# Attention: maxima and scores issued to TensorE in pairs instead of one by one

## The chip, the cores and the metric

One core of a Trainium2 chip. The metric is the device time of one execution of the whole kernel in microseconds; three executions of the kernel before gave 4830.11 to 4836.53 us.

## What is computed

Two layers on a batch of 2 x 2048 tokens of width 512. Only the attention of the first layer is changed; the mixture of experts before and after it and the second layer are not.

```
q = (x @ q_w.T).reshape(b, s, HEADS, HEAD_DIM).transpose(0, 2, 1, 3)
k = x @ k_w.T
v = x @ v_w.T
scores = jnp.einsum('bhqd,bkd->bhqk', q, k) * SCALE
attn = jax.nn.softmax(scores.astype(jnp.float32), axis=-1).astype(q.dtype)
out = jnp.einsum('bhqk,bkd->bhqd', attn, v)
```

There are 16 heads of 32, and all heads share one set of keys and values. b is 2, s is 2048.

## The kernel before

The program is a sequence of stages written out per engine, with semaphores set by hand: experts, projection, `attention_stage` (L1125), output, experts, feed-forward, key-value mixing, feed-forward. `attention_stage` works on 128 queries and 8 heads at a time, which the code calls a half; there are 2 x 16 x 2 = 64 halves. Softmax needs the largest score of each query and head before the exponential, so each half's scores are computed twice, in two layouts:

- A **maximum** (`maxi`, L1237) is a matmul with the queries of one head as weights and 512 keys moving. It fills one of four PSUM banks `am` (`MBANKS`). DVE reduces the bank to one column (L1386). `am_bank` (L1216) makes a matmul wait for the use of its bank four uses before: a maximum's reduction, or, where that use was a transpose, the copies out of it.
- A **turn** (L1249): once per half, the negated maxima are transposed by a small matmul into an `am` bank of their own turn in the ring; DVE copies them out (L1400, L1402, `mT_kept`), and SP puts them as two more rows beside the queries (L1197), so that the score matmul subtracts them.
- A **score** (`score`, L1224) is a matmul with 128 keys as weights and four heads of 128 queries moving. It fills one of three banks `sc` (`SBANKS`), and waits in `p_rdy` for the exponential of the score three before it. ACT computes the exponential (L1338) into a ring of eight units `pt`.
- The **values** (L1255): 16 matmuls a batch multiply the exponentials with v. **Sums** (L1264): POOL adds the units in pairs (L1373), DMAs fold them, and once per half 8 matmuls sum them over the keys (L1267). DVE takes reciprocals (L1411) and scales the output (L1418).

TensorE's order is written out by hand in a loop over batches `c` of four units (L1278). A batch consists of 8 maxima, for scores that come 28 units later (`LEAD`), and 8 scores, one by one in turn, called m0, s0, m1, s1, ... m7, s7 below, then the values of four units. 56 maxima run ahead of the first score. Four batches make a half. In one of the four, called the turned batch here, the turn stands behind m3; the other three are called plain, and one of these has the sums ahead of its values. A pair m, s or a single one of them is called a piece, and the sixteen places of the pieces in a batch are slots 0 to 15.

Of the kernel before, what the change touches and what calls it, by code (L numbers as in the profile page):

```python
# [1110 lines left out]
BATCH = 4  # L1111
SBANKS, MBANKS = 3, 4
LEAD = 28
# [11 lines left out]
def attention_stage(nc, stage, const, q_parts, kst, v, attn, o_w, w_hi, w_lo):  # L1125
# [6 lines left out]
    with ExitStack() as ctx:  # L1132
# [26 lines left out]
        PIECES_ALL = 2 * N * UNITS  # L1159
# [4 lines left out]
        def turn_due(c, i):  # L1164

            half, at = divmod(c + 3, PER_HALF)
            return half if at == 0 and i == 3 and 0 <= half < HALVES else None
# [10 lines left out]
        def slot(half, j):  # L1178

            return 2 * (half % SETS) + j if j < 2 else 2 * SETS + j - 2  # L1180

        @block.sync
        def _(sp):
            def load(x):
                n, h = divmod(x, 2)
                k = n % 2
                for r, part in enumerate((0, 0, 1)):
                    src = q_parts[part, h * HALF * HD:(h + 1) * HALF * HD, n * P:(n + 1) * P].rearrange("(h d) q -> d h q", d=HD)
                    sp.dma_start(qst[r * HD:(r + 1) * HD, k, h * HALF:(h + 1) * HALF, :].bitcast(F32), src).then_inc(q_in[k][h], 16)

            def maxima(x):

                n, h = divmod(x, 2)
                sp.wait_ge(mT_kept, x + 1)
                for part in range(2):
                    row = KROWS + part
                    sp.dma_start(qst[row:row + 1, n % 2, h * HALF:(h + 1) * HALF, :].bitcast(F32),  # L1197
                                 mT[:, part, :].bitcast(F32)).then_inc(m_in[h], 16)

            for x in range(4):  # L1200
                load(x)
            for c in range(DC):
                sp.dma_start(raw[:, c, :], o_w[:, c, :]).then_inc(w_in, 16)
            maxima(0)
            for x in range(HALVES):
                if x + 1 < HALVES:
                    maxima(x + 1)
                if x + 4 < HALVES:
                    sp.wait_ge(s_rdy, HPIECES * (x + 1))
                    load(x + 4)  # L1210

        @block.tensor
        def _(pe):
            pe.sem_inc(p_rdy, SBANKS)

            def am_bank(use):  # L1216

                k = am_slot[use]
                if k >= MBANKS:
                    kind, which = am_use[k - MBANKS]  # L1220
                    pe.wait_ge(mx_rdy if kind == "max" else mT_kept, which + 1)
                return k % MBANKS

            def score(s):  # L1224

                half, r = divmod(s, HPIECES)
                n, h = divmod(half, 2)
                kt, g = divmod(r, 2)
                if r == 0:
                    pe.wait_ge(m_in[h], n * 32 + 32)  # L1230
                pe.wait_ge(p_rdy, s + 1)
                hh = h * HALF + g * 4
                o = (n // QT) * S + kt * P
                pe.matmul(sc[:, s % SBANKS, :], kst[0:KROWS + 2, o:o + P], qst[0:KROWS + 2, n % 2, hh:hh + 4, :],  # L1234
                          start=True, stop=True).then_inc(s_rdy, 1)

            def maxi(a):  # L1237

                half, r = divmod(a, HPIECES)
                n, h = divmod(half, 2)  # L1240
                hd, block = divmod(r, KBLOCKS)
                if r == 0:
                    pe.wait_ge(q_in[n % 2][h], (n // 2) * 48 + 48)
                bank = am_bank(("max", a))
                o = (n // QT) * S + block * 4 * P
                pe.matmul(am[:, bank, :], qst[0:KROWS, n % 2, h * HALF + hd, :], kst[0:KROWS, o:o + 4 * P],  # L1246
                          start=True, stop=True).then_inc(am_rdy, 1)

            def turn(half):  # L1249

                pe.wait_ge(neg_rdy, half + 1)
                bank = am_bank(("turn", half))
                pe.transpose(am[0:HALF, bank, 0:P], neg[:], const["ident"][:]).then_inc(mT_rdy, 1)

            def values(u):  # L1255
                half, kt = divmod(u, QT)
                n = half // 2
                pe.wait_ge(p_rdy, SBANKS + 2 * u + 2)
                for j in range(4):
                    ins = pe.matmul(pv[HD * j:HD * (j + 1), 0, :], v[:, (n // QT) * QT + kt, :], pt[:, u % RING, 2 * P * j:2 * P * (j + 1)],  # L1260
                                    start=(kt == 0), stop=(kt == QT - 1), skip_group_check=True)
                ins.then_inc(pv_rdy, 1)

            def add_up(half, j, first, last):  # L1264

                for i in range(4):
                    ins = pe.matmul(pv[HD * i:HD * (i + 1), 1, :], const["ones"][:, 0:HD], pairs[:, slot(half, j), 2 * P * i:2 * P * (i + 1)],  # L1267
                                    start=first, stop=last, skip_group_check=True)
                if last:
                    ins.then_inc(sum_rdy, 1)  # L1270

            def sums(half):

                pe.wait_ge(fold_in[-1], 16 * (half + 1))
                for j in range(2):
                    add_up(half, j, False, j == 1)

            for c in range(-LEAD // BATCH, BATCHES):  # L1278
                if c == 0:
                    for s in range(SBANKS):  # L1280
                        score(s)
                for i in range(2 * BATCH):
                    a, s = 2 * (c * BATCH + LEAD) + i, 2 * c * BATCH + SBANKS + i
                    if a < PIECES_ALL:
                        maxi(a)
                    if turn_due(c, i) is not None:
                        turn(turn_due(c, i))
                    if c >= 0 and s < PIECES_ALL:
                        score(s)
                if c < 0:  # L1290
                    continue
                half, at = divmod(c, PER_HALF)
                if at == 0 and half >= 1:
                    pe.wait_ge(vals_kept, half)
                if at == 1 and half >= 2:
                    pe.wait_ge(sums_kept, half - 1)
                if at == 0 and half >= 2:
                    sums(half - 2)
                for u in range(c * BATCH, (c + 1) * BATCH):
                    values(u)  # L1300
            pe.wait_ge(vals_kept, HALVES)
            sums(HALVES - 2)
            pe.wait_ge(sums_kept, HALVES - 1)
            for j in range(HPAIRS):
                pe.wait_ge(pair_rdy, RING // 2 + (HALVES - 1) * HPAIRS + j + 1)
                add_up(HALVES - 1, j, j == 0, j == HPAIRS - 1)
# [1133 lines left out]
```

## Time and profile before

| | us |
|---|---|
| median of 3 executions | 4834.5 |
| lowest, highest | 4830.11, 4836.53 |
| profiled execution, its own time | 4831.27 |
| its span | 4829.6 |
| attention, first to last score | 985.7 to 2544.0 |
| one half (four batches) in the middle of it | 24.36 |

The span is the time from the first to the last instruction that the profiler saw. Busy time is counted per engine: PE is TensorE's matmuls, PEld its weight loads, which run beside matmuls. Matmuls overlap each other too, so what tells their pace is the distance of their starts, and not their length.

### The profile page before, as it was taken

The page shows a single profiled execution, that of the slowest core. Times are in us where ns is not written, and L with a number is a line of the kernel's source. Part 1 is how long each engine was busy: PE and PEld are TensorE (multiplying, and loading weights), DVE is VectorE, ACT ScalarE, POOL GpSimd, SP SyncE. Part 2 cuts the span into 40 slices and gives each one's busy share as a digit, 9 for nine tenths or more (in the row PEclk, how much of TensorE's full clock was granted, in tenths as well). Part 3 has the DMA queues.
Part 4 walks back from the last instruction along what each step waited for, and adds up shares of the span by engine and source line. Part 5 has one row for each costly group of instructions (what it writes and reads, how often), then busy time and mean ns, then how long its engine had stood idle before and what let it go on. Part 6 is the DMA issues. An engine that isn't in the chain of part 4 may idle for free. (4 is left out here: it accounts for less than half of the span.)

```text
span 4829.6 us, 82831 instructions
## 1 busy us (share of the span) xinstructions
PE 4626.9 (96%) x27966; PEld 3477.5 (72%) x27967; DVE 2897.6 (60%) x5285; ACT 2107.7 (44%) x4111; POOL 2258.1 (47%) x1724
## 2 busy tenths in 40 slices
PE   6999996999999999999998799999899999999999
PEld 4788885666666666666656578888788877778888
DVE  6222225799999999999974722333455548754444
ACT  4222223456676666776662422222322235533222
POOL 1545433278888888888881154543111007500000
PEclk8999998999999999999999799999999999999999
DMA  7233326757777777777764733433522112250110
GB/s 220 83 93 98 93 83 213 260 104 146 148 146 147 146 146 147 147 147 147 146 135 155 231 94 122 131 119 110 179 66 70 55 51 82 70 196 27 35 35 27
DMA packets 245975, 585.69 MB, mean 121 GB/s; under 512 B 30816, under 2 KB 85088, under 8 KB 221152
## 3 DMA queue, kind: packets, MB, share of 16 engines
q0 software_dynamic: 62064, 317.23, 29.2%
q1 hardware_dynamic: 183536, 263.86, 16.7%
q8 instruction: 186, 3.05, 0.3%
q14 instruction: 189, 1.55, 0.1%
HBM read 263.27 MB, written 121.63 MB: 80 GB/s over the span
## 5 line engine op out<-in xcount | busy, mean ns | idle before, releaser
L1373 POOL TENSOR_TENSOR attend_pairs<-attend_pt 128x1024 f32<-128x1024 f32 x512 | 1259.0, 2478 | 197.4 <-ACT attend_pt L1338 197.2
L1386 DVE TENSOR_REDUCE attend_mx<-attend_am_ps 128x1 f32<-128x512 f32 x2048 | 1251.0, 678 | 124.7 <-PE attend_am_ps L1246 121.4
L1338 ACT ACTIVATE attend_pt<-attend_sc_ps 128x512 f32<-128x512 f32 x2048 | 1039.9, 618 | 285.3 <-PE attend_sc_ps L1234 285.1
L1246 PE MATMUL attend_am_ps<-attention_kst,attend_qst 96*128 96x512 f32 x2048 | 859.1, 425 | 10.2 <-DMA attend_qst<-q_parts 10.1
L1234 PE MATMUL attend_sc_ps<-attend_qst,attention_kst 98*128 98x512 f32 x2048 | 816.7, 400 | 1.5 <-ACT attend_pt L1338 1.3
L1637 PE MATMUL ffn_gu_ps<-ffn_y_hi,ffn_w 128*128 128x512 f32 (+1 forms) x1584 | 568.8, 369 | 3.5 <-DVE ffn_y_lo L1767 3.0
L1637 PE MATMUL ffn_gu_ps<-ffn_y_lo,ffn_w 128*128 128x512 f32 (+1 forms) x1584 | 569.0, 369 | 0.0
L1246 PEld LDWEIGHTS attend_am_ps<-attention_kst,attend_qst 96*128 96x128 f32 x2048 | 392.8, 192 | 239.8 <-DVE attend_mx L1386 122.8
L1260 PE MATMUL attend_pv_ps<-attend_pt,attention_v 128*32 128x256 f32 x8192 | 497.6, 384 | 0.0
L741 DVE TENSOR_TENSOR expert_ac<-expert_gu_ps,expert_gl 128x512 f32<-128x512 f32 x142 | 98.1, 691 | 640.5 <-ACT expert_gl L698 640.5
L1234 PEld LDWEIGHTS attend_sc_ps<-attend_qst,attention_kst 98*128 98x128 f32 x2048 | 389.4, 190 | 88.7 <-ACT attend_pt L1338 11.7
L1260 PEld LDWEIGHTS attend_pv_ps<-attend_pt,attention_v 128*32 128x32 f32 x8192 | 247.6, 110 | 214.1 <-ACT attend_pt L1338 46.8
L1709 ACT ACTIVATE ffn_sg<-ffn_gu_ps,ffn_gs 128x512 f32<-128x512 f32 (+1 forms) x198 | 127.2, 642 | 581.7 <-PE ffn_gu_ps L1637 581.7
L698 ACT ACTIVATE expert_gl<-expert_gu_ps 128x512 f32<-128x512 f32 x142 | 85.1, 599 | 661.3 <-PE expert_gu_ps L635 659.9
L635 PE MATMUL expert_gu_ps<-weights_hi,expert_x_hi 128*128 x1088 | 355.1, 408 | 5.8 <-DVE expert_x_lo L737 3.2
L635 PE MATMUL expert_gu_ps<-weights_lo,expert_x_hi 128*128 x1088 | 343.7, 397 | 0.0
L635 PE MATMUL expert_gu_ps<-weights_hi,expert_x_lo 128*128 x1088 | 343.4, 397 | 0.0
L1637 PEld LDWEIGHTS ffn_gu_ps<-ffn_y_hi,ffn_w 128*128 128x128 f32 x1584 | 298.4, 188 | 61.2 <-DVE ffn_y_lo L1767 3.6
L1637 PEld LDWEIGHTS ffn_gu_ps<-ffn_y_lo,ffn_w 128*128 128x128 f32 x1584 | 298.4, 188 | 57.4
L1777 DVE SCALAR_TENSOR_TENSOR ffn_hf<-ffn_gu_ps,ffn_us,ffn_sg 128x512 f32<-128x512 f32 (+1 forms) x198 | 137.0, 692 | 330.9 <-PE ffn_gu_ps L1637 323.1
L745 DVE TENSOR_TENSOR expert_a_lo<-expert_at_ps,expert_a_hi 128x512 fp32r<-128x512 f32 x142 | 98.1, 691 | 307.3 <-ACT expert_a_hi L702 307.3
L1653 PE MATMUL ffn_dn_ps<-ffn_w,ffn_h_hi 128*128 128x512 f32 x704 | 279.0, 396 | 0.0
(329 smaller groups left out, 7725.6 us busy)
## 6 DMA issues: line engine op xcount, KB each, us to landing
attend_pairs<-attend_pairs POOLq DMA_DIRECT2D x189, 1024.0 KB, 7.4
weights_raw<-experts_dram POOLq DMA_DIRECT2D x76, 512.0 KB, 4.1
ys<-expert_ob SPq DMA_DIRECT2D x142, 256.0 KB, 2.2
attend_qst<-q_parts SPq DMA_DIRECT2D x192, 128.0 KB, 3.9
yn<-route_yb SPq DMA_DIRECT2D x64, 256.0 KB, 4.1
ffn_xb<-x SPq DMA_DIRECT2D x64, 256.0 KB, 2.9
keyvalue_xb<-x SPq DMA_DIRECT2D x64, 256.0 KB, 2.8
weights_lo<-experts_dram SPq DMA_DIRECT2D x24, 512.0 KB, 9.5
```

Source lines behind the costliest of these rows:

```text
L635: ins = pe.matmul(gu[:, q, :], a, w[:, bass.ds(off + (c * WPIECE + q * H), H)], start=(c == 0 and n == 0), stop=(c == DC - 1 and n == 2))
L741: dve.tensor_tensor(ac[:, k, :], gu[:, 1, :], gl[:, k, :], ALU.mult).then_inc(ac_rdy, 1)
L1234: pe.matmul(sc[:, s % SBANKS, :], kst[0:KROWS + 2, o:o + P], qst[0:KROWS + 2, n % 2, hh:hh + 4, :], start=True, stop=True).then_inc(s_rdy, 1)
L1246: pe.matmul(am[:, bank, :], qst[0:KROWS, n % 2, h * HALF + hd, :], kst[0:KROWS, o:o + 4 * P], start=True, stop=True).then_inc(am_rdy, 1)
L1260: ins = pe.matmul(pv[HD * j:HD * (j + 1), 0, :], v[:, (n // QT) * QT + kt, :], pt[:, u % RING, 2 * P * j:2 * P * (j + 1)], start=(kt == 0) ...
L1338: act.activation(pt[:, u % RING, g * 4 * P:(g + 1) * 4 * P], sc[:, s % SBANKS, :], ACT.Exp, scale=HD ** -0.5).then_inc(p_rdy, 1)
L1373: pool.tensor_tensor(pairs[:, slot(half, j), :], pt[:, 2 * p % RING, :], pt[:, (2 * p + 1) % RING, :], ALU.add).then_inc(pair_rdy, 1)
L1386: dve.tensor_reduce(mx[:, hh, block:block + 1], am[:, am_slot["max", a] % MBANKS, :], AX.X, ALU.max).then_inc(mx_rdy, 1)
L1637: ins = pe.matmul(gu[:, k, q, 0:width], a, b, start=(c == 0 and n == 0), stop=(c == DC - 1 and n == 1))
L1653: ins = pe.matmul(dn[:, j % 2, :], a, b, start=(m == 0 and n == 0), stop=(m == IC - 1 and n == 1))
L1709: act.activation(sg[:, k, 0:n], gu[:, k, 0, 0:n], ACT.Silu, scale=gs[:, m:m + 1]).then_inc(sg_rdy, 1)
L1777: dve.scalar_tensor_tensor(hf[:, k, 0:n], gu[:, k, 1, 0:n], us[:, m:m + 1], sg[:, k, 0:n], ALU.mult, ALU.mult).then_inc(h_rdy, 1)
```

## The change

In a batch two maxima are issued and then two scores. The turn stays directly behind m3. No other engine's code is touched.

```diff
-                for i in range(2 * BATCH):
-                    a, s = 2 * (c * BATCH + LEAD) + i, 2 * c * BATCH + SBANKS + i
-                    if a < PIECES_ALL:
-                        maxi(a)
-                    if turn_due(c, i) is not None:
-                        turn(turn_due(c, i))
-                    if c >= 0 and s < PIECES_ALL:
-                        score(s)
+                for first in range(0, 2 * BATCH, 2):
+                    for i in (first, first + 1):
+                        a = 2 * (c * BATCH + LEAD) + i
+                        if a < PIECES_ALL:
+                            maxi(a)
+                        if turn_due(c, i) is not None:
+                            turn(turn_due(c, i))
+                    for i in (first, first + 1):
+                        s = 2 * c * BATCH + SBANKS + i
+                        if c >= 0 and s < PIECES_ALL:
+                            score(s)
```

On PE, in a turned batch from m2 on, before (`attend_am_ps<-attention_kst` is a maximum, `attend_sc_ps` a score, L1253 the turn):

```order
L1246 MATMUL attend_am_ps<-attention_kst,attend_qst 128x512
L1234 MATMUL attend_sc_ps<-attend_qst,attention_kst 128x512
L1246 MATMUL attend_am_ps<-attention_kst,attend_qst 128x512
L1253 MATMUL attend_am_ps<-all_ident,attend_neg 8x128
L1234 MATMUL attend_sc_ps<-attend_qst,attention_kst 128x512
L1246 MATMUL attend_am_ps<-attention_kst,attend_qst 128x512
L1234 MATMUL attend_sc_ps<-attend_qst,attention_kst 128x512
```

The same place now, from m2 to s7 and the values:

```order
L1246 MATMUL attend_am_ps<-attention_kst,attend_qst 128x512 x2
L1253 MATMUL attend_am_ps<-all_ident,attend_neg 8x128
L1234 MATMUL attend_sc_ps<-attend_qst,attention_kst 128x512 x2
L1246 MATMUL attend_am_ps<-attention_kst,attend_qst 128x512 x2
L1234 MATMUL attend_sc_ps<-attend_qst,attention_kst 128x512 x2
L1246 MATMUL attend_am_ps<-attention_kst,attend_qst 128x512 x2
L1234 MATMUL attend_sc_ps<-attend_qst,attention_kst 128x512 x2
L1260 MATMUL attend_pv_ps<-attend_pt,attention_v 32x256 x16
```

s2 has moved behind m3 and the turn; the turn is followed by two scores instead of one.

On PE, the end of a plain batch before (m6, s6, m7, s7 and the values):

```order
L1246 MATMUL attend_am_ps<-attention_kst,attend_qst 128x512
L1234 MATMUL attend_sc_ps<-attend_qst,attention_kst 128x512
L1246 MATMUL attend_am_ps<-attention_kst,attend_qst 128x512
L1234 MATMUL attend_sc_ps<-attend_qst,attention_kst 128x512
L1260 MATMUL attend_pv_ps<-attend_pt,attention_v 32x256 x16
```

And now, from m4 on:

```order
L1246 MATMUL attend_am_ps<-attention_kst,attend_qst 128x512 x2
L1234 MATMUL attend_sc_ps<-attend_qst,attention_kst 128x512 x2
L1246 MATMUL attend_am_ps<-attention_kst,attend_qst 128x512 x2
L1234 MATMUL attend_sc_ps<-attend_qst,attention_kst 128x512 x2
L1260 MATMUL attend_pv_ps<-attend_pt,attention_v 32x256 x16
```

Between the last maximum and the values stand two scores where there was one. The order on DVE, ACT, POOL and SP is the same before and after.

## Rows read from the trace of the kernel before

**Rows 1.** The page's engine shares: busy us (share of the span) x instructions.

```profile
PE 4626.9 (96%) x27966; PEld 3477.5 (72%) x27967; DVE 2897.6 (60%) x5285; ACT 2107.7 (44%) x4111; POOL 2258.1 (47%) x1724
```

**Rows 2.** Windows: length, busy of PE, PEld, DVE, ACT, POOL, clock, DMA, GB/s.

```profile
1400.00:1800.00 400.00, 400.00 (x3436) 260.85 (x3429) 368.17 (x656) 279.05 (x558) 352.73 (x181) 1.00 0.72 147
...
1504.87:1529.23 24.36, 24.36 (x213) 15.88 (x209) 22.48 (x40) 17.01 (x34) 21.53 (x11) 1.00 0.73 146
```

**Rows 3.** Groups by line, 1000 to 2400 us: busy us, mean ns | idle before, releaser.

```profile
L1386 DVE TENSOR_REDUCE attend_mx<-attend_am_ps 128x1 f32<-128x512 f32 x1840 | 1124.2, 678 | 106.3 <-PE attend_am_ps L1246 103.2
L1338 ACT ACTIVATE attend_pt<-attend_sc_ps 128x512 f32<-128x512 f32 x1840 | 934.3, 617 | 237.1 <-PE attend_sc_ps L1234 237.1
```

**Rows 4.** Timeline of a plain batch: start us, length, engine, instruction, [idle before <-releaser].

```profile
1535.35 0.50 PE L1246 MATMUL attend_am_ps<-attention_kst,attend_qst 96*128 96x512 f32 x1
1535.68 0.40 PE L1234 MATMUL attend_sc_ps<-attend_qst,attention_kst 98*128 98x512 f32 x1
1535.88 4.87 DVE L1386 TENSOR_REDUCE attend_mx<-attend_am_ps 128x1 f32<-128x512 f32 x8 [0.28 <-PE attend_am_ps L1246]
...
1536.12 4.03 ACT L1338 ACTIVATE attend_pt<-attend_sc_ps 128x512 f32<-128x512 f32 x8 [1.93 <-PE attend_sc_ps L1234]
...
1538.95 0.39 PE L1234 MATMUL attend_sc_ps<-attend_qst,attention_kst 98*128 98x512 f32 x1
...
1539.27 1.93 PE L1260 MATMUL attend_pv_ps<-attend_pt,attention_v 128*32 128x256 f32 x32
...
1541.13 0.50 PE L1246 MATMUL attend_am_ps<-attention_kst,attend_qst 96*128 96x512 f32 x1
```

**Rows 5.** Timeline of the turned batch before it.

```profile
1529.23 0.50 PE L1246 MATMUL attend_am_ps<-attention_kst,attend_qst 96*128 96x512 f32 x1
...
1529.77 2.48 DVE L1386 TENSOR_REDUCE attend_mx<-attend_am_ps 128x1 f32<-128x512 f32 x4 [1.47 <-PE attend_am_ps L1246]
...
1531.71 0.19 PEld L1246 LDWEIGHTS attend_am_ps<-attention_kst,attend_qst 96*128 96x128 f32 x1 [0.19 <-DVE attend_mx L1386]
...
1531.79 0.43 PE L1246 MATMUL attend_am_ps<-attention_kst,attend_qst 96*128 96x512 f32 x1
...
1532.48 0.28 DVE L1402 TENSOR_TENSOR attend_mT<-attend_am_ps,attend_mT 8x128 fp32r<-8x128 f32 x1
...
1532.81 0.19 PEld L1246 LDWEIGHTS attend_am_ps<-attention_kst,attend_qst 96*128 96x128 f32 x1 [0.20 <-DVE attend_mT L1402]
...
1532.89 0.42 PE L1246 MATMUL attend_am_ps<-attention_kst,attend_qst 96*128 96x512 f32 x1
...
1533.15 0.40 PE L1234 MATMUL attend_sc_ps<-attend_qst,attention_kst 98*128 98x512 f32 x1
```

**Rows 6.** Timeline of a batch of scores alone, near the end of attention.

```profile
2503.93 0.96 PE L1234 MATMUL attend_sc_ps<-attend_qst,attention_kst 98*128 98x512 f32 x3
2504.47 4.03 ACT L1338 ACTIVATE attend_pt<-attend_sc_ps 128x512 f32<-128x512 f32 x8
...
2505.12 0.19 PEld L1234 LDWEIGHTS attend_sc_ps<-attend_qst,attention_kst 98*128 98x128 f32 x1 [0.53 <-ACT attend_pt L1338]
2505.12 2.46 PE L1234 MATMUL attend_sc_ps<-attend_qst,attention_kst 98*128 98x512 f32 x5
```

**Rows 7.** Timeline of the batch with the sums: first maximum, first reductions.

```profile
1546.95 0.50 PE L1246 MATMUL attend_am_ps<-attention_kst,attend_qst 96*128 96x512 f32 x1
...
1547.59 3.07 DVE L1386 TENSOR_REDUCE attend_mx<-attend_am_ps 128x1 f32<-128x512 f32 x5
```

**Rows 8.** Windows: maxima alone ahead of the first score, and scores alone in the tail.

```profile
952.00:985.00 33.00, 32.03 (x56) 15.71 (x56) 31.38 (x55) 3.47 (x5) 4.96 (x4) 0.50 0.26 64
...
2530.37:2534.50 4.13, 3.91 (x27) 1.61 (x29) 3.25 (x5) 4.03 (x9) 3.39 (x3) 1.00 0.00 0
```

**Rows 9.** Timeline at the start of the first batch, at the lower clock.

```profile
987.81 0.63 PE L1234 MATMUL attend_sc_ps<-attend_qst,attention_kst 98*128 98x512 f32 x1
...
988.23 0.63 PE L1246 MATMUL attend_am_ps<-attention_kst,attend_qst 96*128 96x512 f32 x1
```

## Prediction

> **What bounds the kernel now.** Start with the engine shares [rows 1]: PE is busy 96% of the span, but that is an average over eight stages and says nothing about attention, the only stage that changes. Then the windows [rows 2]: between 1400 and 1800 us PE is busy for all 400 us at a granted clock of 1.00, its upper level (2.4 GHz), while DVE, the next busiest, has 368. The third view groups the attention instructions by line [rows 3]: one maximum occupies DVE for 678 ns, one exponential ACT for 617 ns. Eight of each belong to a batch. The last view, instructions in order of time, gives the answer. Four batches (one half) take 24.36 us [rows 2]: one carries the transpose (turned), three don't (plain). In a plain batch [rows 4] the first maximum starts at 1535.35, the second piece 0.33 later, and the sixteenth at 1538.95; so the slots behind the first are (1538.95 - 1535.68) / 14 = 0.2336 us apart without one hole. The values follow 0.32 behind the last piece, and the next batch 1.86 behind them. **TensorE sets the pace there, and whatever delays the last piece delays the whole kernel.** DVE and ACT only matter by the banks that they free, so the question is how close those releases come to the slots that need them.
>
> **The change part by part.** No instruction is added or removed. On DVE, ACT, POOL and SP the order is the same, and the sixteen slots of a batch hold the same work. What moves, counting slots from 0: m1, m3, m5, m7 go one slot forward (2 to 1, 6 to 5, 10 to 9, 14 to 13), s0, s2, s4, s6 one slot back (1 to 2, 5 to 6, 9 to 10, 13 to 14). If nothing waits, the cost is nothing. DMAs: the transposed maxima leave SP after the same DVE copies, and they are needed almost three batches later; the query loads wait for the last score of a half, which is far ahead of use. Both stay free; if a load lost that cover it would show as a wait of the first maximum of a half.
>
> *Prices of a wait.* A maximum waits for the reduction four bank uses before it. In the turned batch [rows 5] the first four reductions take 2.48 us from 1529.77, 0.60 apart, so the third ends at 1531.65; the weight load that needs its bank starts at 1531.71, and its matmul ends at 1531.79 + 0.43 = 1532.22. So a maximum ends no sooner than 0.57 behind its release. For scores I found no such wait between 1000 and 2400 us, so I take it from the tail, where batches hold scores only [rows 6]: the exponential of the first score starts at 2504.47, and the weight load of the score three later, which reuses the bank, starts at 2505.12, which is 0.65 later. The five scores then last 2.46 us at 0.49 each, so one ends 2.46 - 4 x 0.49 = 0.50 behind its load. A score ends no sooner than 1.15 behind the start of the exponential three before it.
>
> *Plain batch*, in us from the start of m0. A piece in slot k ends at 0.33 + 0.2336 (k - 1) + 0.40 [rows 4], slot 15 at 4.00. Now s0 is in slot 1, ends at 0.73, and its exponential starts at 1536.12 - 1535.35 = 0.77; the eight then run in one piece, 0.49 apart. s7 needs the exponential of s4, which starts at 0.77 + 1.96 = 2.73: it could end at 3.88 and ends at 4.00, 0.12 to spare. After the change s0 ends at 0.96, and the chain of exponentials starts at 1.00, one slot later. s3, in slot 7 (end 2.13), could end at 2.15; s5, in slot 11 (end 3.07), is held to 1.00 + 0.98 + 1.15 = 3.13; s7, still in slot 15, is held to 1.00 + 1.96 + 1.15 = 4.11 against 4.00. These delays are of one chain, so the largest counts and not their sum: **0.115 us**. The maxima press less: the reductions start at 0.53, the fourth ends at 0.53 + 1.80 + 0.68 = 3.01, so m7 could end at 3.58, where slot 13 ends at 3.53; the hold of s5 has moved it further already. The batch with the sums is alike: its reductions start 0.64 behind its first maximum now [rows 7], since DVE comes late from the output, but a longer batch gives DVE that time back. There are 249 batches that hold both kinds ((2048 - 56) / 8; 56 maxima run ahead), 62 of them turned. 187 x 0.115 = 21.5 us.
>
> *Turned batch* [rows 5]. The transpose takes a bank too, so m5 is bound by the third reduction and m7 by the copy that ends at 1532.48 + 0.28 = 1532.76; m7's load starts at 1532.81 and m7 at 1532.89. DVE is a running chain from the first reduction, and m0 keeps its slot, so neither release moves. m7 stays at 1532.89. Behind it stands one score now (1533.15); after the change two. **One slot, 0.23 us**, times 62 = 14.3 us. The exponentials don't bind here, since the same waits have delayed the scores.
>
> Two neighbours of one kind could run closer: three scores in a row take 0.96 us [rows 6], hence (0.96 - 0.50) / 2 = 0.23 apart against 0.2336. In the chain that binds, only the step from m0 to m1 and one of the two last would profit: about 1 us in all, left out. The sum is 21.5 + 14.3 = 35.8 us on the profiled execution's 4831.27 us, so 4867.1; that execution is 3.2 below the median of the runs, 4834.5, which becomes **4870**.
>
> **Bounds.** From below: if ACT's releases come just early enough, 0.12 of slack in a chain that I read to 0.01 at best, the plain batches cost nothing and the turned ones remain: +14.3, 4849. From above: every moved slot is exposed in every batch, 249 x 0.2336 = 58.2, 4893. I take the value in the middle because rows 6 measure the same wait in the same code.
>
> **Rivals.**
> 1. *Only the turned batches pay* (4849). For it: the plain batch misses by half a slot. Against: the tail shows the release with no slack. 10%.
> 2. *A whole slot in every batch* (4893), if the first score's late start also holds POOL or the values. Against: the values need the exponential of s4 only for their last unit, and POOL waits for ACT, not ACT for it. 10%.
> 3. *No change*: both releases are hidden by something the timeline doesn't show, so less than 9.7 us. 8%.
> 4. *Faster.* The mechanism: eight of fifteen steps in a batch now join matmuls of one kind, and each could be 0.2336 - 0.23 = 0.004 shorter or better. The waits would have to vanish as well: it decides from the point where exponential and reduction release their banks 0.12 us sooner than rows 5 and 6 say. Then 249 x 8 x 0.004 = 8 us, and with 0.008 per step 16 us: 4819. For it: a score behind a score has the shorter step in rows 6. Against: the chain of exponentials runs from s0 whatever PE does, so PE would only arrive sooner and wait. 4%. The Trainium skill (TensorE: Matmul & The Clock Gate, Back-to-back issue gap) gives 216 ns for an isolated step of 512 columns; by it, estimated, eight steps a batch would save 36 us, but no row of this stage is that short.
> 5. *The clock falls.* At the lower level (1.2 GHz) a step takes 988.23 - 987.81 = 0.42 us [rows 9], so a batch takes 15 x 0.19 = 2.9 us longer; if one batch in ten fell, 25 x 2.9 = 72 us on top: 4943. The clock was 0.50 between 952 and 985 us [rows 8], where PE did one maximum per reduction and idled in between. Against it: score-only batches that wait before every score are granted 1.00 [rows 8], and so are the turned batches with their three waits [rows 2]. 2%. The Trainium skill (same page, A second HAM failure mode: psum-queue depth-cycling) says that short idle gaps between matmul groups that cycle through PSUM banks can make the clock oscillate. By it this change, which adds such gaps, would cost far more than my sum; the rows at 1.00 speak against it.
>
> **How the numbers follow.** Forecast 66% (4860 to 4880 by itself), rivals 10, 10, 8, 4 and 2%. Under 0.2%, 9.7 us, a measurement of this kernel can't tell a change from none. Slower: 66 + 10 + 10 + 2 = 88%. Same 8%, faster 4%. The range 4848 to 4893 holds the forecast and rivals 1 and 2 and takes in both bounds.
>
> **What would show it.** In a plain batch the weight load of the last score waits for ACT, and the values start 3.92 + 0.12 behind m0; four batches take 24.36 + 0.23 + 3 x 0.12 = 24.9 us; in the turned batch m7 starts 3.66 behind m0 as before and the values follow 0.23 later. The exponentials start 1.00 behind m0. Granted clock 1.00 throughout. I am wrong if PE's slots have no hole in plain batches, if the holes stand at maxima there, or if another stage changes its length.

## The result and the profile after

The changed kernel takes 4877.41 us (median of 4, 4872.05 to 4880.24) against 4834.21 us: a ratio of 1.0089, 95% interval 1.0072 to 1.0106, so 43 us slower. The forecast was 4870, which is + 36. Measured again beside the last experiments, the changed kernel took 4877.89 us, a ratio of 1.0090 (1.0074 to 1.0105). The profiled execution took 4880.24 us.

The page's engine shares and two windows in the middle of attention, the second one half long:

```profile
span 4878.6 us, 82831 instructions
...
PE 4673.8 (96%) x27966; PEld 3438.5 (70%) x27967; DVE 2911.7 (60%) x5285; ACT 2122.2 (44%) x4111; POOL 2254.1 (46%) x1724
```

```profile
1400.00:1800.00 400.00, 399.84 (x3341) 242.96 (x3339) 362.04 (x638) 274.71 (x542) 342.80 (x177) 1.00 0.71 143
...
1522.19:1547.29 25.10, 25.07 (x214) 15.25 (x210) 22.71 (x40) 17.24 (x34) 21.47 (x11) 1.00 0.70 142
```

The same instructions run, PE is as busy as before (96%, [rows 1]) and granted the same clock, 1.00; but 400 us hold 3341 matmuls where they held 3436 [rows 2], and a half takes 25.10 us instead of 24.36. The share of busy time says nothing of this: the record of a matmul lasts 0.40 us and the next one starts 0.23 us behind it [rows 4], so a delay of 0.1 us between two starts leaves no idle time.

Who waited for whom between 1000 and 2400 us (us in total, times, longest):

```profile
PEld attend_sc_ps L1234 <- ACT attend_pt L1341: 75.1, 378, 0.2
PEld attend_am_ps L1246 <- issue: 68.8, 167, 0.4
PEld attend_am_ps L1246 <- DVE attend_mx L1389: 67.5, 180, 0.4
...
PEld attend_sc_ps L1234 <- issue: 15.7, 56, 0.3
```

The first row is new: no score waited for an exponential in this stretch before. The last is new too, and it is one score per half: s5 of the batch ahead of the sums is the first score of the next half, and the code makes it wait for its rows of maxima as well as for the exponential (a wait put down to "issue" is one for which the profile shows no releaser). The two middle rows are weight loads of maxima and much as before: together 136 us, where the same two were 123 us (99.9 and 23.5). The timeline of a plain batch (start us, length, engine, instruction, idle before and releaser) shows where:

```profile
1528.52 0.30 PEld L1246 LDWEIGHTS attend_am_ps<-attention_kst,attend_qst 96*128 96x128 f32 x2 [0.41 <-DVE attend_mx L1389]
...
1529.07 4.88 DVE L1389 TENSOR_REDUCE attend_mx<-attend_am_ps 128x1 f32<-128x512 f32 x8 [0.51 <-PE attend_am_ps L1246]
...
1529.54 4.03 ACT L1341 ACTIVATE attend_pt<-attend_sc_ps 128x512 f32<-128x512 f32 x8 [1.92 <-PE attend_sc_ps L1234]
...
1530.19 0.19 PEld L1234 LDWEIGHTS attend_sc_ps<-attend_qst,attention_kst 98*128 98x128 f32 x1 [0.19 <-ACT attend_pt L1341]
...
1531.17 0.19 PEld L1234 LDWEIGHTS attend_sc_ps<-attend_qst,attention_kst 98*128 98x128 f32 x1 [0.22 <-ACT attend_pt L1341]
...
1532.15 0.19 PEld L1234 LDWEIGHTS attend_sc_ps<-attend_qst,attention_kst 98*128 98x128 f32 x1 [0.22 <-ACT attend_pt L1341]
...
1532.58 1.93 PE L1260 MATMUL attend_pv_ps<-attend_pt,attention_v 128*32 128x256 f32 x32
```

m0 starts at 1528.53 (its load at 1528.52); the exponentials start 1.01 behind it, where they started 0.77 behind it [rows 4]. The loads of s3, s5 and s7 wait for ACT, each 0.65, 1.63 and 2.61 us behind the first exponential, so 0.98 apart: two exponentials of 0.49. The values start 4.05 behind m0 instead of 3.92.

In the turned batch ahead of it, whose m0 starts at 1522.19, the load of m7 still waits for the copy of the turn:

```profile
1525.76 0.19 PEld L1246 LDWEIGHTS attend_am_ps<-attention_kst,attend_qst 96*128 96x128 f32 x1 [0.31 <-DVE attend_mT L1405]
...
1526.66 1.93 PE L1260 MATMUL attend_pv_ps<-attend_pt,attention_v 128*32 128x256 f32 x32
```

It starts 3.57 behind m0, where it started 3.58 behind it [rows 5], and the values follow 0.90 behind it instead of 0.67: one slot more.

The batch with the sums holds the surprise:

```profile
1538.54 2.38 POOL L1376 TENSOR_TENSOR attend_pairs<-attend_pt 128x1024 f32<-128x1024 f32 x1
...
1540.35 0.85 DVE L1421 TENSOR_TENSOR attended_attn<-attend_vals,attend_inv 128x256 f32<-128x256 f32 x1
...
1540.36 0.73 PE L1246 MATMUL attend_am_ps<-attention_kst,attend_qst 96*128 96x512 f32 x2
...
1541.13 4.86 DVE L1389 TENSOR_REDUCE attend_mx<-attend_am_ps 128x1 f32<-128x512 f32 x8
...
1543.65 0.19 PEld L1246 LDWEIGHTS attend_am_ps<-attention_kst,attend_qst 96*128 96x128 f32 x1 [0.37 <-DVE attend_mx L1389]
...
1544.00 0.63 PE L1234 MATMUL attend_sc_ps<-attend_qst,attention_kst 98*128 98x512 f32 x2
```

The reductions start 0.77 behind m0, not 0.64 as before [rows 7] and not earlier as I had said, because DVE's output multiply took 0.85 us. So the load of m7 waits for DVE there. The time that the longer batches give DVE is in it: the multiply starts 0.01 ahead of m0, where it started 0.09 behind it (1547.04 against 1546.95). But it is 0.23 longer, which leaves the reductions 0.13 later. Over the stage (one row per kernel, the multiply by its tile; count, min/median/max ns; before, then changed):

```profile
L1418 DVE TENSOR_TENSOR attended_attn<-attend_vals,attend_inv x56: 620/628/711, 1059.7 to 2399.9; 128x256 f32<-128x256 f32 x56
```

```profile
L1421 DVE TENSOR_TENSOR attended_attn<-attend_vals,attend_inv x54: 852/859/874, 1063.6 to 2393.3; 128x256 f32<-128x256 f32 x54
```

To take attention apart from the rest, I use its **body**, from the first maximum to the last transpose. Kernel before, then changed (tile of the maxima: count, min/median/max ns, first and last start):

```profile
L1246 PE MATMUL attend_am_ps<-attention_kst,attend_qst x2048: 392/397/797, 952.7 to 2500.6; 96*128 96x512 f32 x187
...
L1253 PE MATMUL attend_am_ps<-all_ident,attend_neg x64: 272/273/374, 973.7 to 2504.7; 128*8 128x128 f32 x64
```

```profile
L1246 PE MATMUL attend_am_ps<-attention_kst,attend_qst x2048: 387/396/796, 954.1 to 2547.1; 96*128 96x512 f32 x187
...
L1253 PE MATMUL attend_am_ps<-all_ident,attend_neg x64: 272/275/372, 975.1 to 2551.3; 128*8 128x128 f32 x64
```

The body grows from 2504.7 - 952.7 = 1552.0 to 2551.3 - 954.1 = 1597.2 us, + 45.2; in the second execution of the changed kernel that was profiled it is 2551.7 - 954.7 = 1597.0. Behind the body the kernel varies by itself: from the last transpose to the first matmul of the output stage it takes 2606.1 - 2551.3 = 54.8 us in one and 2601.5 - 2551.7 = 49.8 us in the other execution of the same kernel. That is why the body is the sharper measure below, though each body is that of one profiled execution.

### The profile page after: what moved, and what is told of

The parts are those of the page before. It is cut to its first block and busy times, and to the rows that moved or that the text cites. A ratio compares the mean times of both kernels' runs of the same rounds, so it can differ in the third digit from the quotient of the medians.

```text
span 4878.6 us, 82831 instructions
## 1 busy us (share of the span) xinstructions
PE 4673.8 (96%) x27966; PEld 3438.5 (70%) x27967; DVE 2911.7 (60%) x5285; ACT 2122.2 (44%) x4111; POOL 2254.1 (46%) x1724
## 5 line engine op out<-in xcount | busy, mean ns | idle before, releaser
L1341 ACT ACTIVATE attend_pt<-attend_sc_ps 128x512 f32<-128x512 f32 x2048 | 1054.1, 610 | 332.5 <-PE attend_sc_ps L1234 323.6
L1246 PE MATMUL attend_am_ps<-attention_kst,attend_qst 96*128 96x512 f32 x2048 | 723.0, 428 | 10.4 <-DMA attend_qst<-q_parts 9.6
L1234 PE MATMUL attend_sc_ps<-attend_qst,attention_kst 98*128 98x512 f32 x2048 | 676.9, 410 | 1.5 <-ACT attend_pt L1341 1.3
L1246 PEld LDWEIGHTS attend_am_ps<-attention_kst,attend_qst 96*128 96x128 f32 x2048 | 372.7, 191 | 252.4 <-DVE attend_mx L1389 90.7
```

What stands on the lines that cost most here:

```text
L1341: act.activation(pt[:, u % RING, g * 4 * P:(g + 1) * 4 * P], sc[:, s % SBANKS, :], ACT.Exp, scale=HD ** -0.5).then_inc(p_rdy, 1)
```

## Experiments

In all of them the batches are measured between starts of first maxima, from 1500 to 1610 us of the profile, in the order turned, plain, plain, sums, each the mean of four or five; the body as above; the time against the kernel before on the same chip. Theory of the releases: a piece is late where its PSUM bank is released late, and only the latest such piece of a batch counts. Main rival: neighbours of one kind cost time as such. For the sums batch, whose 0.26 us I had not forecast, a second pair: POOL's late add holds DVE, or the batch is long by itself.

| kernel | batches, us | body, us | time against before |
|---|---|---|---|
| before | 6.10, 5.80, 5.80, 6.66 | 1552.0 | 1 |
| changed | 6.34, 5.91, 5.93, 6.92 | 1597.2 | 1.0089 |
| changed, again | 6.34, 5.91, 5.93, 6.91 | 1597.0 | 1.0090 |
| e1 turned batch in pairs | 6.33, 5.79, 5.81, 6.66 | 1566.8 | 1.0028 (1.0017 to 1.0039) |
| e2 first pair only | 6.10, 5.90, 5.92, 6.77 | 1574.0 | 1.0045 (1.0029 to 1.0062) |
| e3 batch ahead of the sums | 6.10, 5.81, 5.92, 6.69 | 1562.5 | 1.0017 (1.0007 to 1.0026) |
| e4 batch with the sums | 6.10, 5.80, 5.80, 6.81 | 1562.4 | 1.0013 (1.0004 to 1.0023) |
| e5 all pairs but the first | 6.34, 5.87, 5.88, 6.72 | 1580.3 | 1.0051 (1.0035 to 1.0066) |
| e6 changed, output later | 6.34, 5.91, 5.92, 6.77 | 1587.9 | 1.0081 (1.0066 to 1.0097) |
| e6 again | 6.34, 5.91, 5.93, 6.77 | 1587.8 | 1.0061 (1.0048 to 1.0075) |
| e7 changed, short exponentials | 6.33, 5.83, 5.83, 6.79 | 1578.2 | 1.0042 (1.0026 to 1.0057) |
| e9 changed, short adds | 6.33, 5.91, 5.92, 6.77 | 1587.9 | 1.0096 (1.0078 to 1.0114) |
| e9 again | 6.34, 5.91, 5.93, 6.77 | 1588.7 | 1.0085 (1.0072 to 1.0099) |
| e8 before, turned tail | 5.95, 5.80, 5.80, 6.68 | 1543.9 | 0.9984 (0.9975 to 0.9993) |

The order of pieces is a string in e1 to e5 and e8, with at = 1 in the turned batch and 0 in the one with the sums (here e1):

```diff
-                for i in range(2 * BATCH):
+                at = c % PER_HALF
+                for piece in "mmss" * 4 if at == 1 else "ms" * 8:
```

**e1**

> Pairs in the turned batch alone, the three others one by one. Theory of the releases: m7 starts 3.66 us behind m0 as in the kernel before and one more score stands behind it, so the turned batch takes 6.12 + 0.22 = 6.34 us, the others stay at 5.78, 5.82 and 6.65 us, a half takes 24.58 us, and the whole is 62 x 0.22 = 14 us over the kernel before. Rival (neighbours of one kind cost time as such, the same in every batch): a quarter of the change's 43 us, 11 us, and the extra time lies spread over the batch and not behind m7.

The turned batch took 6.33 us, the others stayed; the body grew by 14.8 us and the median by 12.6 (4845.14 against 4832.58). This is what the releases forecast: one slot behind a held m7. In time alone the rival's 11 us lies inside the interval too; the batches decide, since it wants 0.17 us on every paired batch (43 / 249) and nothing like the 0.23 seen in this one.

**e2**, `"mmss" + "ms" * 6`:

> Only the first pair of each batch: m0 m1 s0 s1, then one by one. Theory of the releases: s0 is a slot later, so the chain of exponentials is, and s7 is held by its whole 0.115 us though one pair of four is left; the first exponential still starts 1.00 us behind m0. Turned batch unchanged (m7 is held as before and has one score behind it). POOL's adds start a slot later too, so in the batch with the sums the reductions start 0.77 us behind m0 and the batch is 0.12 us longer. A half 24.36 + 3 x 0.115 = 24.7 us, the whole + 21 us. Rival (neighbours cost as such): a quarter of the change, + 11 us, the turned batch 0.06 us longer as well.

This is the sharpest one. A quarter of the same-kind neighbours costs the plain batches 5.90 + 5.92 against 5.80 + 5.80, 0.11 each, nearly all of what the whole change costs them, and the turned batch nothing. The body grew by 22.0 us, the median by 21.3 (4853.87 against 4832.58). What costs in plain batches is that **the first score is a slot later**: one pair out of four costs as much as all four. The loads of s3 to s6 in one of its batches with the sums, from the timeline, all wait, 0.49 us apart, which is ACT's pace:

```profile
1532.32 0.19 PEld L1234 LDWEIGHTS attend_sc_ps<-attend_qst,attention_kst 98*128 98x128 f32 x1 [0.20 <-ACT attend_pt L1344]
1532.81 0.19 PEld L1234 LDWEIGHTS attend_sc_ps<-attend_qst,attention_kst 98*128 98x128 f32 x1 [0.19 <-ACT attend_pt L1344]
1533.30 0.19 PEld L1234 LDWEIGHTS attend_sc_ps<-attend_qst,attention_kst 98*128 98x128 f32 x1 [0.19 <-ACT attend_pt L1344]
1533.79 0.19 PEld L1234 LDWEIGHTS attend_sc_ps<-attend_qst,attention_kst 98*128 98x128 f32 x1 [0.19 <-ACT attend_pt L1344]
```

**e3 and e4**, `at == 3` and `at == 0` in place of `at == 1`:

> Pairs only in the batch ahead of the one with the sums. Theory: that batch takes 0.10 us longer (5.92); its exponentials and with them POOL's two adds are a slot later, DVE's output multiply lies 0.85 us instead of 0.63 behind POOL's add, and the reductions of the batch with the sums, itself unchanged, start 0.77 us behind m0 instead of 0.64: m7 there could end at 3.82 and its slot ends at 3.77, so + 0.05 us. A half 24.51 us, the whole + 9 us. Rival (the long multiply belongs to the batch with the sums itself): the multiply stays at 0.63 us, + 6 us.

> Pairs only in the batch with the sums. Theory: the multiply stays at 0.63 us and the reductions at 0.64 us behind m0, m7 could end at 0.64 + 2.48 + 0.57 = 3.69 and its slot now ends at 3.53, so this batch takes 0.16 us longer (6.81), the others nothing; the whole + 10 us. Rival (the batch with the sums costs the 0.28 us that it does in the changed kernel by itself): 6.93 us, the whole + 17 us.

```profile
L1424 DVE TENSOR_TENSOR attended_attn<-attend_vals,attend_inv x55: 850/864/878, 1061.9 to 2385.7; 128x256 f32<-128x256 f32 x55
```

```profile
L1424 DVE TENSOR_TENSOR attended_attn<-attend_vals,attend_inv x55: 624/625/699, 1060.8 to 2384.7; 128x256 f32<-128x256 f32 x55
```

The multiply is long (first row, e3) where the batch *ahead* of the sums is in pairs, and short (second row, e4) where the sums batch itself is. Its own pairs cost that batch 0.15 us, not 0.26, and the long multiply alone costs it 0.03. Together they cost more than the sum of the two, since before the change m7 had some slack there: it could end at 0.64 + 2.48 + 0.57 = 3.69 and ended at 3.77. That slack can be used up once only. Bodies grew by 10.5 and 10.4 us where + 9 and + 10 were forecast. The medians grew by only 5.1 and 6.2 us; their intervals, 3 to 13 and 2 to 11 us, hold the growth of the bodies.

**e5**, `"msms" + "mmss" * 3`:

> m0 s0 m1 s1 as before, then pairs. Theory of the releases: s0 keeps its slot, the exponentials start 0.77 us behind m0 and POOL's adds when they did; s2 is late, so the chain from there is 0.15 us late and s7 is held by 0.07 us in a plain batch, m7 by 0.05; the turned batch is 0.22 us longer as in the changed kernel; the batch with the sums 0.09 us. A half 24.36 + 0.14 + 0.22 + 0.09 = 24.8 us, the whole + 28 us; the multiply stays at 0.63 us. Rival (neighbours cost as such): three quarters of the change, + 32 us, with plain batches 0.09 us longer.

Turned and plain batches as forecast; the sums batch cost 0.06 us and not 0.09. The body grew by 28.3 us, the median by 27.5 (4856.03 against 4828.53). With s0 in its old slot the multiply lasts 0.62 us in spite of three pairs in every batch, so of the pairs it is the first that lengthens it. The longer batches now do give DVE time back: the reductions of the sums batch start 0.56 behind m0 and not 0.64. That is why this batch cost less than forecast.

**e6**, the changed kernel with the multiply a batch later:

```diff
-                    if at == 2:
+                    if at == 3:
                         output(half)
+            output(HALVES - 3)
```

> The changed kernel with DVE's output multiply a batch later, behind the maxima of the batch with the sums, where DVE waits for TensorE anyway. Theory: the reductions of the batch with the sums start 0.53 us behind m0 instead of 0.77, m7 is free and only the exponentials hold s7, so that batch falls from 6.93 to 6.77 us, and nothing else changes: 62 x 0.16 = 10 us below the changed kernel, 33 us over the one before. Rival (what makes that batch long is the score chain or the sums): no change against the changed kernel, + 43 us.

The sums batch fell to 6.77 us, to the hundredth, and the body by 9.3 us. The whole took 4868.73 us, 9 us less than the changed kernel on another chip, and the interval (1.0066 to 1.0097) holds the changed kernel's 1.0089. So the two were measured once more on one chip:

> The changed kernel again, on the same chip as the next two, so that the three can be compared: 62 x 0.74 = 46 us by its batches, 43 us as measured first. Sums batch 6.93 us, multiply 0.86 us.

> The later output multiply again. Theory: 62 x 0.15 = 9 us below the changed kernel on the same chip. Rival (the gain seen in the batch is given back elsewhere): the same time as the changed kernel.

4861.84 against 4877.89 us, 16 us faster, with a body 9.2 us shorter. No execution of the one (4860.39 to 4863.33) reaches those of the other (4869.16 to 4879.01), so the gain reaches the end. What it is over 9 us isn't the body's: of the 15.4 us between the two profiled executions 2.9 lie ahead of the first maximum and 3.3 behind the last transpose, where the kernel varies by itself.

**e7**, the changed kernel with half of each exponential (half of the attention weights stay uncomputed):

```diff
+                w = 4 * P if s < 2 * RING else 2 * P
```

> The changed kernel with exponentials over half of each bank from the seventeenth on: half of the exponentials are left out, so this is a probe and not a version. Theory: with ACT quick no score waits; in a plain batch m7 alone is held, by 0.05 us, so it takes 5.83 us instead of 5.92; the turned batch is as in the changed kernel (6.34), since DVE holds it; POOL starts sooner, so the batch with the sums takes 6.77 us. A half 24.8 us, the whole + 27 us. Rival (plain batches are long because of the order on TensorE itself): plain batches stay at 5.92 us.

Plain batches fell to 5.83 us, turned and sums batches are within 0.02 us of the forecast: ACT's pace is what holds plain batches, and with it gone DVE's 0.03 us shows. The body is + 26.2 us. The whole was + 20.5 us (4849.02 against 4828.53) and not + 27. I had left out the tail, where batches of scores alone run at ACT's pace [rows 6]: from the last transpose to the first matmul of the output stage it takes 45.1 us here, 52.9 in the kernel before and 47.9 or more in every other run. These 7.8 us are of single executions and are as much as is missing.

**e9**, the changed kernel with POOL's adds over half of the columns (half of the softmax sums are left out):

```diff
+                w = HALF * P if half < SETS else HALF * P // 2
```

> The changed kernel with POOL's adds over half of the columns from the fourth half on: half of the sums is left out, so this is a probe. Theory: DVE's output multiply ends 0.28 us behind the POOL add that runs when it starts, in both kernels; without such an add it takes 0.42 us, as in the tail of the kernel before, so the reductions of the batch with the sums start 0.53 us behind m0 again and that batch falls from 6.93 to 6.77 us; plain and turned batches stay at 5.92 and 6.34 us. The whole 62 x 0.16 = 10 us below the changed kernel. Rival (the multiply is long because DVE itself runs late, POOL has no part): multiply 0.85 us, batch 6.93 us, no change.

```profile
L1422 DVE TENSOR_TENSOR attended_attn<-attend_vals,attend_inv x54: 424/426/850, 1059.8 to 2382.0; 128x256 f32<-128x256 f32 x54
```

The multiply takes 0.43 us and the sums batch 6.77: here the add that used to run beside the multiply has ended before it starts. With e3, where a late add lengthens the multiply of a batch that is itself unchanged, this shows that POOL's add was the cause. But four executions (4868.18 to 4881.51 us) showed no gain in the whole, so:

> Half of POOL's adds again, since four executions that lay 13 us apart did not say whether the 0.15 us that the batch with the sums loses reaches the end. Theory: 62 x 0.15 = 9 us below the changed kernel on the same chip, and some us more from the tail, where POOL's adds are the longest work. Rival (given back elsewhere): the same time as the changed kernel.

Again a body 8.3 us shorter than the changed kernel's, and again the same time: 4874.39 against 4877.89 us, where 9 us or more were expected. The traces show a loss behind attention. Matmuls of the second experts stage, changed kernel and then this one (count, min/median/max ns, first and last start):

```profile
L635 PE MATMUL expert_gu_ps<-weights_hi,expert_x_hi x544: 388/398/791, 2816.4 to 3446.3; 128*128 x182
```

```profile
L635 PE MATMUL expert_gu_ps<-weights_hi,expert_x_hi x552: 388/398/791, 2812.8 to 3457.3; 128*128 x184
```

With half of the sums missing, attention's output is another one, and tokens are routed to experts by it: 552 matmuls in this group instead of 544, 644.5 us instead of 629.9 (in the first run of e9 552 too, and 639.9 us). That loss is the probe's own, behind the place that it probes, and as large as the gain looked for or larger. So e9 shows the gain in the body only; that it reaches the end is shown by e6.

**e8**, a version of the kernel before, `"ms" * 6 + "smsm" if at == 1 else "ms" * 8`:

> The kernel before, with the end of the turned batch alone reordered: from m6 on it is s6 m6 s7 m7. Theory: the third and fourth reduction and the copy of the turn free their banks so that m5, m6 and m7 could end at 2.98, 3.58 and 4.09 us behind m0; in slots 10, 13 and 15 behind the turn they end at 2.96, 3.67 and 4.13 anyway, so nearly all of the 0.19 us of holes in this batch goes: 5.95 us instead of 6.12, the whole 62 x 0.17 = 10 us under the kernel before, 4824 us. Rival (the holes come back elsewhere, as s6 and s7 a slot sooner wait for ACT): no gain.

The end of its turned batch (weight loads, matmuls, DVE):

```profile
1530.02 0.19 PEld L1246 LDWEIGHTS attend_am_ps<-attention_kst,attend_qst 96*128 96x128 f32 x1 [0.19 <-DVE attend_mx L1392]
...
1530.49 0.19 PEld L1234 LDWEIGHTS attend_sc_ps<-attend_qst,attention_kst 98*128 98x128 f32 x1 [0.17 <-ACT attend_pt L1344]
...
1530.79 0.28 DVE L1408 TENSOR_TENSOR attend_mT<-attend_am_ps,attend_mT 8x128 fp32r<-8x128 f32 x1
...
1531.31 0.39 PE L1246 MATMUL attend_am_ps<-attention_kst,attend_qst 96*128 96x512 f32 x1
...
1531.63 1.93 PE L1260 MATMUL attend_pv_ps<-attend_pt,attention_v 128*32 128x256 f32 x32
```

m5 waits for the third reduction as before (first row), but m6 and m7 no longer wait for DVE; s6 (second row) and s7 now wait for ACT, for some hundredths. The batch takes 5.95 us instead of 6.10, and the batch with the sums 6.68 instead of 6.66. The whole takes 4820.63 against 4828.53 us over 11 and 15 executions, 0.16% faster with an interval that excludes no change. That is less than the 10 us forecast, as the body's 8.1 us is, and **faster than both kernels**.

## Why the prediction was right, and where it was not

The time lies in the range (4848 to 4893), 7 us over the forecast; the likeliest case came in, and the sum was 35.8 us where the body shows 45.2 and the whole 43. Rival 1 (plain batches cost nothing) and rival 3 (no change) are out by the plain batches' 0.12 us and by the interval. A half takes 25.10 us and not 24.9.

- *TensorE sets the pace, no cost if nothing waits*: held. e7 leaves four pairs in every batch and takes the waits for ACT away, and plain batches come within 0.03 us of the old length.
- *Plain batch, 0.115 us, a chain that starts a slot late*: held. Measured (5.91 + 5.93 - 5.80 - 5.80) / 2 = 0.12; the exponentials start 1.01 behind m0 (forecast 1.00); s3, s5 and s7 are the ones that wait. e2 shows that s0's slot is the cause, and e5, where s2 is the first late score, costs 0.07 by the same chain.
- *Turned batch, one slot, 0.23 us*: held, 0.24; m7 is still released by the copy, at the same time, and e1 shows it alone.
- *The batch with the sums is alike, "a longer batch gives DVE that time back"*: **this step failed.** It cost 0.26 and not 0.115 us, 62 x 0.145 = 9 us, which is the whole difference between sum and body. I had DVE's multiply at a fixed length. It isn't: it ends behind the POOL add that runs when it starts, and that add follows another that waits for the first exponential of its batch, so it is a slot later as well. DVE did get 0.10 us back from the longer batches, but the multiply took 0.23 more. The reductions start late, m7 is held to 0.77 + 2.48 + 0.57 = 3.82, and slot 13 ends at 3.53: + 0.29, measured 0.26. The hole of this batch stands at a maximum, which I had named as a sign of being wrong. I had rejected rival 2 with "POOL waits for ACT, not ACT for it"; that is true, but DVE waits for POOL, and this batch lost more than the slot that was my upper bound. The total stayed in the range because the plain batches cost only half a slot.
- *Even at the multiply's old length* e4 measures 0.15 in that batch: with the reductions 0.64 behind m0 the same formula gives 0.64 + 2.48 + 0.57 - 3.53 = 0.16. The numbers for it stood in rows 7; I waved them off.
- *Clock*: the granted clock was 1.00 from 1000 to 2500 us before and after, with three waits in each plain batch. Rival 5 is out: these waits of about 0.2 us did not bring the clock down. Rival 4 is out too: it needed waits to vanish, and waits for ACT were added.

## What to carry to other kernels

Where one engine runs without holes, write down for each bank the slot that needs it and the earliest time that its release allows; a reorder costs the largest shortfall in a batch, not their sum, and a late *first* item shifts the whole chain of its consumer. Follow every consumer one step further: POOL's add hung on the same exponential, and DVE on the add. And a probe that changes data must be read up to the first place whose work depends on the data.

## What the runs showed of the hardware that I had not expected

DVE's multiply of two SBUF tensors, 128 x 256, takes 0.42 to 0.43 us alone (e9), and beside a POOL add of two SBUF tensors it lasts to 0.28 us behind that add's end. Before, POOL's pair of adds from 1542.65 ends at 1547.38 and the multiply at 1547.66; after the change 1540.92 and 1541.20; in e6, where it starts 0.93 us ahead of the add's end, it takes 1.21 us:

```profile
1537.87 4.71 POOL L1376 TENSOR_TENSOR attend_pairs<-attend_pt 128x1024 f32<-128x1024 f32 x2 [0.39 <-ACT attend_pt L1341]
```

```profile
1541.65 1.21 DVE L1421 TENSOR_TENSOR attended_attn<-attend_vals,attend_inv 128x256 f32<-128x256 f32 x1
```

POOL ends at 1542.58, the multiply at 1542.86, 0.28 behind it once more. The three multiplies start 0.34, 0.57 and 0.93 us ahead of the add's end and take 0.62, 0.85 and 1.21 us: each us of overlap costs a whole us, so the two do not share, one waits. DVE's reductions, which read PSUM, keep their 0.60 us step beside the same adds. The Trainium skill (SBUF — State Buffer, SBUF: two separate sides) says that a DVE instruction with two SBUF inputs and a GpSimd one that reads SBUF take one shared pair of ports as an exclusive lock, and that the later one waits. By that rule the multiply must wait for the add; the traces agree, with 0.28 us from the add's end to the multiply's. That is 0.14 us less than the multiply takes alone, so a part of its length passes before or beside the wait; which part, no trace here shows.
